# Queries and keys of a windowed attention projected three batches ahead instead of two

## The reference

```python
q = (x @ wq + bq).reshape(B, S, NH, HD)...      # 16 heads of 8; k and v likewise
for i in range(0, S, w2):                        # windows of 64 tokens, 32 apart
    qw = q[:, start:end] * scale
    attn = softmax(qw @ kw^T);  wo = attn @ vw
    out = ... blended with a linear ramp where two windows overlap
...
out = ctx @ wproj + bproj + residual             # then layer norm, gelu MLP, residual
```

## Time and profile before

| what | before |
|---|---|
| three runs, us | 391.68, 396.9, 400.08 |
| median, us | 396.9 |
| profiled execution, us | 393.26 |
| its span, us | 391.5 |
| PE busy | 298.5 us, 76% |
| DVE busy | 226.1 us, 58% |
| ACT busy | 141.4 us, 36% |
| POOL busy | 78.1 us, 20% |
| DMA, moved | 22.98 MB, mean 59 GB/s |
| granted PE clock, mean | 0.80 |

### The profile page before, as it was taken

One profiled execution on the slowest core, in us unless ns is written; L12 is line 12 of the kernel. 1 busy time (PEld: TensorE's weight loads), 2 busy tenths in 40 slices (PEclk: granted clock), 3 DMA queues, 4 the chain that ended last, 5 costly groups with the idle time before them and its releaser, 6 DMA issues.

```text
span 391.5 us, 10964 instructions
## 1 busy us (share of the span) xinstructions
PE 298.5 (76%) x4194; PEld 232.2 (59%) x4194; DVE 226.1 (58%) x632; ACT 141.4 (36%) x282; POOL 78.1 (20%) x116
## 2 busy tenths in 40 slices
PE   6363769848769958657576687689889798999993
PEld 4132646736547836536455576556558687878893
DVE  6453506617525426428227254256888689879886
ACT  2243034235314334415322413516544622742310
POOL 4343002203103104104002001003353002302020
PEclk9865587688855568959857856869989899999998
DMA  6019370470650650731812905100000000000000
GB/s 181 14 46 188 78 130 2 126 99 4 145 79 4 140 82 5 174 47 43 167 18 74 150 3 183 43 1 2 0 2 1 0 3 0 28 1 0 28 27 29
DMA packets 39057, 22.98 MB, mean 59 GB/s; under 512 B 4832, under 2 KB 37984, under 8 KB 39008
## 3 DMA queue, kind: packets, MB, share of 16 engines
q1 hardware_dynamic: 39008, 22.28, 27.1%
HBM read 13.88 MB, written 8.13 MB: 56 GB/s over the span
## 4 chain that ended last, share of the span: by engine, by line
PE 38%; DVE 17%; DMA 16%; SPq 13%; issue 10%; ACT 3%; POOL 1%; DVEq 0%; ACTq 0%; POOLq 0%
DMA qst<-stack_scratch 11%; SPq L279 5%; DMA stack_scratch<-parts 5%; SPq L299 5%; PE bank L400 5%; PE bank L658 5%; SPq L291 3%; DVE xh L1027 3%; PE bank L640 3%; PE bank L439 3%; DVE acc L1358 2%; PE bank L641 2%; PE bank L642 2%; PE bank L369 2%; PE bank L492 2%
## 5 line engine op out<-in xcount | busy, mean ns | idle before, releaser
L1068 DVE TENSOR_REDUCE nm<-bank 128x8 f32<-128x512 f32 x64 | 43.2, 688 | 71.1 <-PE bank L400 70.8
L400 PE MATMUL bank<-kst,qst 48*64 48x64 bf16 x1024 | 35.7, 226 | 43.2 <-DMA qst<-stack_scratch 30.8
L400 PEld LDWEIGHTS bank<-kst,qst 48*64 48x64 bf16 x1024 | 28.7, 136 | 57.4 <-issue 56.5
L875 POOL TENSOR_TENSOR rs<-ve,mhalf 128x2 f32<-128x2 f32 (+1 forms) x24 | 19.9, 828 | 169.7 <-DVE ve L1024 162.5
L741 ACT ACTIVATE prob<-bank 128x512 f32<-128x512 f32 x64 | 36.7, 601 | 31.6 <-PE bank L416 31.3
L658 PEld LDWEIGHTS bank<-wds,hh 128*128 128x128 f32 x256 | 32.3, 191 | 7.2 <-issue 5.6
L416 PE MATMUL bank<-qst,kst 50*64 50x64 bf16 x1024 | 29.6, 207 | 8.5 <-issue 4.7
L658 PE MATMUL bank<-wds,hh 128*128 128x128 f32 x256 | 33.7, 277 | 2.9 <-DVE acc L1358 2.4
L827 ACT ACTIVATE sg<-bank 128x512 f32<-128x512 f32 x32 | 19.0, 600 | 45.0 <-PE bank L642 45.0
L1358 DVE SCALAR_TENSOR_TENSOR acc<-bank,rt,acc 128x128 f32<-128x128 f32 x112 | 32.6, 340 | 1.1
L416 PEld LDWEIGHTS bank<-qst,kst 50*64 50x64 bf16 x1024 | 23.6, 120 | 13.8 <-issue 11.5
(11 more groups left out here) (140 smaller groups left out, 508.0 us busy)
## 6 DMA issues: line engine op xcount, KB each, us to landing
qst<-stack_scratch SPq DMA_DIRECT2D x32, 192.0 KB, 4.9
stack_scratch<-parts SPq DMA_DIRECT2D x16, 216.0 KB, 2.5
kst<-stack_scratch SPq DMA_DIRECT2D x16, 216.0 KB, 4.9
stack_scratch<-parts SPq DMA_DIRECT2D x16, 144.0 KB, 2.3
stack_scratch<-parts SPq DMA_DIRECT2D x16, 72.0 KB, 2.7
qst<-mt SPq DMA_DIRECT2D x64, 4.0 KB, 2.2
out_x<-fin SPq DMA_DIRECT2D x4, 256.0 KB, 2.3
xs<-in_x SPq DMA_DIRECT2D x1, 896.0 KB, 7.7
```

What stands on the lines that cost most here:

```text
L400: m = pe.matmul(psa[g % 2][WIN * half:WIN * half + WIN, WIN * h2:WIN * h2 + WIN], qst[n][eo][rows_, h2, at - 32 * eo:at - 32 * eo + WIN], ...
L1068: dve.tensor_reduce(nm[:, g, :], psa[g % 2][:].rearrange("p (h k) -> p h k", h=H2), AX_X, ALU.max, negate=True).then_inc(max_done, 1)
```

## The change

Queries and keys are projected three batches ahead, into three sets of stacks (`DEEP = 3`). In step b, `transpose_x`, `project_qk`, `copy_xt`, `copy_qk`, `cut_qk`, `copy_x1v` and `write_parts` work on batch b + 3; `read_stacks` and `project_v` stay at batch b + 2; the layer norm moves to b + 4. The prologue takes over the projection of batch 2 and the norm of batch 3. On SP the read now stands between the two writes of maxima, and the write of parts behind them. The scratch tensor gets an order in which the eight heads of one row of a stack lie in one run (the columns of wq and wk are permuted on the host to suit), and the query stacks keep all 288 columns. The maxima are transposed as two blocks of 32 rows and written as runs of 256 columns. All eight steps are written out, the counters kept for the loop go, and of 13 added matmuls a step 9 stay (20 become 10 in the prologue). `h3t` and `hh` share memory with the stacks. `ln2_stats` stands before `normalise(b, 0)`.

```diff
 TERMS = 6
+DEEP = 3
...
+        mp = sb("mp", [P, 2, 2, 2, H2], BF16)
+        mt = sb("mt", [4 * H2, S], BF16)
         prob = [sb(f"prob{i}", [P, H2, 2, WIN]) for i in range(2)]
         pvs = sb("pvs", [P, 4, P])
...
             vb = [attention.enter_context(nc.sbuf_tensor(f"vb{i}", [P, 2, NH, 2, 2, VC], F32)) for i in range(2)]
-            qst = [[attention.enter_context(nc.sbuf_tensor(f"qst{i}{eo}", [P, H2, S], BF16)) for eo in range(2)]
-                   for i in range(2)]
-            kst = [attention.enter_context(nc.sbuf_tensor(f"kst{i}", [P, H2, LINE], BF16)) for i in range(2)]
+            qst = [[attention.enter_context(nc.sbuf_tensor(f"qst{i}{eo}", [P, H2, LINE], BF16)) for eo in range(2)]
+                   for i in range(DEEP)]
+            kst = [attention.enter_context(nc.sbuf_tensor(f"kst{i}", [P, H2, LINE], BF16)) for i in range(DEEP)]
...
-        scr = nc.dram_tensor("stack_scratch", [B, P, TERMS, 2, LINE], BF16, kind="Internal").ap()
-        scr_rows = scr.rearrange("b (r h d) t k n -> b r k (d t) h n", r=2, h=H2)
+        scr = nc.dram_tensor("stack_scratch", [B, 2, TERMS, P, LINE], BF16, kind="Internal").ap()
...
             def write_parts(b):
                 sp.wait_ge(parts_step, after(parts_step, 3 * (b + 1)))
-                apart(sp)
-                dst = scr[ds(b, 1)].rearrange("b p t k n -> (b p) t k n")
                 for t0, n, k, src in ((0, 3, 0, parts[:, 0:1, 0, :].broadcast_to([P, 3, LINE])),
...
                                       (5, 1, 1, parts[:, 0:1, 1, :])):
-                    sp.dma_start(dst[:, t0:t0 + n, k, :], src).then_inc((q_written, k_written)[k], 16)
-
...
+                    dst = scr[b, k].rearrange("t p n -> p t n")
+                    sp.dma_start(dst[:, t0:t0 + n, :], src).then_inc((q_written, k_written)[k], 16)
+
+            def read_stacks(b):
+                n = b % DEEP
+                if b >= DEEP:
+                    sp.wait_ge(b_done, after(b_done, 8 * (b - DEEP + 1)))
+                for k, stack, written in ((0, qst[n][0], q_written), (1, kst[n], k_written),
+                                          (0, qst[n][1], q_written)):
                     sp.wait_ge(written, after(written, 48 * (b + 1)))
-                    apart(sp)
+                    rows_of = scr[b, k].rearrange("t (d h) n -> (t d) h n", h=NH)
                     for r in range(2):
-                        src = scr_rows[ds(b, 1), r, k, :, :, cols].rearrange("b r h n -> (b r) h n")
-                        sp.dma_start(stack[64 * r:64 * r + ROWS], src).then_inc(stack_ready, 16)
...
+            def write_mrow(b, hf):
                 sp.wait_ge(mt_ready, after(mt_ready, 2 * b + hf + 1))
-                apart(sp)
                 for par in range(2):
                     for part in range(2):
-                        r, at = 64 * par + ROWS + part, 32 * part + 16 * par
-                        sp.dma_start(qst[n][hf][r:r + 1].rearrange("o h (s q) -> o (h s) q", s=2),
-                                     mt[at:at + 16, :]).then_inc(mrow_ready, 16)
+                        r, at = 64 * par + ROWS + part, 16 * part + 8 * par
+                        sp.dma_start(qst[b % DEEP][hf][r:r + 1, :, 32 * hf:32 * hf + S], mt[at:at + 8, :]
+                                     ).then_inc(mrow_ready, 16)
...
+            sp.wait_ge(ones_ready, after(ones_ready, 2 * DEEP))
+            read_stacks(0)
             write_parts(1)
-            write_mrow(0, 0, 0)
-            read_stacks(1, 1)
+            write_mrow(0, 0)
+            read_stacks(1)
...
+            def step(b):
+                write_mrow(b, 1)
+                if b == 0:
+                    write_parts(2)
+                elif b + 2 < B:
+                    read_stacks(b + 2)
+                if b + 1 < B:
+                    write_mrow(b + 1, 0)
+                if b == 0:
+                    read_stacks(2)
+                if b + 3 < B:
+                    write_parts(b + 3)
+                if b == B - 2:
                     load_late()
-            steps(sp, step)
+            for b in range(B):
+                step(b)
...
+                                      qst[n][eo][rows_, h2, at:at + WIN], kst[n][rows_, h2, at:at + WIN],
                                       start=True, stop=True)
...
-                pe.transpose(bank[0:64, 0:64].bitcast(BF16), mp[:].rearrange("p a c -> p (a c)"), idb[:]
-                             ).then_inc(mt_done, 1)
-
-            def probs_v(b, n, gp):
-
-
+                for sel in range(2):
+                    m = pe.transpose(bank[0:32, 64 * sel:64 * sel + 64].bitcast(BF16),
+                                     mp[:, sel].rearrange("p c a h -> p (c a h)"), idb[:])
+                m.then_inc(mt_done, 1)
...
             pe.wait_ge(mod_ready, after(mod_ready, 2 * B))
             for g in range(5):
-                scores_a(0, 0, g)
+                scores_a(0, g)
             transpose_m(0, 0, w1b)
+            pe.wait_ge(v_ready, after(v_ready, 4))
+            transpose_x(2)
             for g in range(5, 8):
-                scores_a(0, 0, g)
-            pe.wait_ge(v_ready, after(v_ready, 4))
-            project_v(1, 1, 0)
-            project_v(1, 1, 1)
+                scores_a(0, g)
             pe.wait_ge(mt_ready, after(mt_ready, 1))
-            keep_busy(20)
-            scores_b(0, 0, 0)
-            scores_b(0, 0, 1)
...
+            project_qk(2)
+            pe.wait_ge(qk_ready, after(qk_ready, 12))
+            project_v(1, 0)
+            project_v(1, 1)
+            keep_busy(10)
+            scores_b(0, 0)
+            scores_b(0, 1)
...
+            def step(b):
+                ahead, prep, values = b + 1 < B, b + 3 < B, b + 2 < B
...
-                scores_b(b, n, 3)
+                probs_v(b, 0)
+                scores_b(b, 3)
                 a(0)
-                keep_busy(3)
+                keep_busy(2)
                 a(1)
                 if prep:
                     pe.wait_ge(v_ready, after(v_ready, 4 * (b + 2)))
-                    transpose_x(b + 2)
+                    transpose_x(b + 3)
                 a(2)
                 if not ahead:
                     turn_tokens(0)
-                probs_v(b, n, 1)
+                probs_v(b, 1)
                 if prep:
                     pe.wait_ge(att_ready, after(att_ready, b))
-                    project_qk(b + 2, n)
+                    project_qk(b + 3)
...
                 keep_busy(2)
                 a(4)
                 if ahead:
                     if prep:
-                        pe.wait_ge(qk_ready, after(qk_ready, 4 * (b + 3)))
+                        pe.wait_ge(qk_ready, after(qk_ready, 4 * (b + 4)))
...
-                probs_v(b, n, 2)
-                scores_b(b, n, 6)
-                if prep:
-                    project_v(b + 2, n, 0)
+                probs_v(b, 2)
+                scores_b(b, 6)
+                if values:
+                    pe.wait_ge(v_ready, after(v_ready, 4 * (b + 2)))
+                    project_v(b + 2, 0)
                 a(5)
...
+                scores_b(b, 7)
+                if values:
+                    project_v(b + 2, 1)
                 a(6)
...
                 a(7)
                 turn_sums(b, 1)
-                keep_busy(8)
+                keep_busy(5)
...
-                dve.tensor_copy(mt[:], (psa[0] if hf else w1b)[0:64, 0:64].bitcast(BF16)).then_inc(mt_ready, 1)
+                dve.tensor_copy(mt[:], (psa[0] if hf else w1b)[0:32, 0:128].bitcast(BF16)).then_inc(mt_ready, 1)
...
-            for n in range(2):
+            for n in range(DEEP):
...
+            ln_a(3)
             for g in range(5):
                 maxima(0, g)
             copy_mt(0, 0)
+            ln_b(3)
             for g in range(5, 8):
                 maxima(0, g)
...
+            ln_c(3)
+            cut_qk(2, 0)
+            cut_qk(2, 1)
+            ln_d(3)
...
                 maxima_next(2)
                 maxima_next(3)
-                normalise(b, 0)
                 if group is not None:
                     ln2_stats(group)
+                normalise(b, 0)
                 if norm:
...
                 if prep:
-                    cut_qk(b + 2, 0)
+                    cut_qk(b + 3, 0)
                 if ahead:
                     copy_mt(b + 1, 0)
                 if prep:
-                    cut_qk(b + 2, 1)
+                    cut_qk(b + 3, 1)
...
     vmask[P - PAD:, 1, 1] = 0
+    by_dim = np.arange(D).reshape(NH, HD).T.reshape(D)
```

More of the change, by code:

```diff
@@ L607, in step @@
                 project_out(b)
-            steps(pe, step)
+            for b in range(B):
+                step(b)
             def second(g, c):
@@ L1217, in step @@
                     ln2_stats(NG - 1)
-            steps(dve, step)
+            for b in range(B):
+                step(b)
             normed_tokens(NG - 1)
```

199 lines of the change are left out of this document (88 added, 111 removed).

## The result

| | us, median (lowest to highest, runs) | profiled execution | ratio to before, 95% interval |
|---|---|---|---|
| before | 398.49 (391.68 to 400.69, 4) | 393.26, span 391.5 | |
| after | 343.45 (339.89 to 346.75, 4) | 342.37, span 340.6 | 0.868 (0.8486 to 0.8875) |

The kernel became 13% faster: 343.45 us against 349 forecast, with a range of 335 to 366. In the profiled executions the span falls by 50.9 us: 2.3 before the first scores of batch 1 (57.55 became 55.2), 41.3 in the six steps behind it (168.05 became 126.8), and 7.3 from there to the end (165.9 became 158.6). The forecast was added up from a profiled execution: -44.3 us, beside these -50.9.

A forecast was written before the change was run, and what follows sets the result against it. The tensor engine, busy 76% of the span, waited once per step for the DMA reading the stacks. Six steps -43.1, prologue +0.3, step 6 -1.5: -44.3 from the profiled 393.26, so 349 us, range 335 to 366.

The forecast's parts named there:

- The stall: Waits of scores_a for the DMA reading the stacks, 30.8 us in seven waits; claimed gone in steps 1 to 5.
- The middle steps: Steps 1 to 4, claimed at 21.2 - 0.6 + 0.3 = 20.9 us each, with 30% of the time at the lower clock.
- The line behind it: Step time without the stall: 19.3 us plus 6.4 us times the share of time at the lower clock.
- Rival 1: Full clock everywhere: 19.0 us per middle step, 337 us in all; chance 12%.
- Not the row of maxima: Row write before scores_b(b, 4): claimed not the next wait, with 2.5 us of slack, 0.6 after a warm start.
- Rival 3: The row of maxima becomes the wait, behind the reads on SP: 2.5 us lost per step, 364 us; chance 9%.
- The chain through DVE: Vector engine from first normalisation to end of ln_d: next late, gather_context waits for it; part of the 19.3 us, kept.
- Fewer added matmuls: 13 per step become 9, before gather_context: -0.6 us a step, bounds 0 and -1.0.
- Rival 2: The clock stays low because eight matmuls before gather_context become five: 24.1 us a step, 370 us; chance 12%.
- One run per row: Stack reads move runs of eight heads at once; hidden from step 1 on, worth nothing in the sum but room.
- Step 0: Stacks of batch 2, still read in this step, arrive 22.0 us into it: +1.1 against 20.9, bounds 0 and +3.
- Behind the last first scores: Steps 6 and 7 and all behind 250 us: same work, -1.5 us for a warmer start, bounds 0 and -4.

The follow-up runs named there:

- e2: The changed kernel with projections two batches ahead, two sets of stacks and SP's old order, the rest of the change kept; 374.37 us.
- e8: The changed kernel with SP reading the stacks of batch b+2 at the end of step b, behind the part writes, in steps 1 to 5; 363.88 us.
- e6: The changed kernel with the row of maxima written in two DMAs of two rows instead of four of one row; 334.23 us.
- e9: The changed kernel with parts of batch 2 written in the prologue and the row of maxima written in two DMAs; 329.82 us.
- e3: The changed kernel with the scratch tensor in its old order, reads in runs of 576 bytes; 350.22 us.
- e7: The changed kernel with one more DVE addition of 128x512 float32 in each of the eight steps; 341.54 us.
- e12: The changed kernel with three more DVE additions of 128x512 float32 in each of the eight steps; 350.33 us.
- e4: The changed kernel with the added matmuls of before, 3, 2 and 8 a step and 20 in the prologue; 343.77 us.
- e5: The changed kernel with the parts of batch 2 written in the prologue, behind the reads of batch 1, instead of in step 0; 338.05 us.
- e1: The kernel before with its eight steps written out and nothing else changed; 391.69 us, ratio 0.9833.
- e11: The changed kernel with five more added matmuls in each step, in front of scores_a(b+1, 6); 342.03 us.

## Why the prediction was right

*The stall* went as said. No first `scores_a` of batches 1 to 7 waits for its stacks; even the exceptions named, batches 1 and 2, were none. e2 shows that the distance does it, e8 that it does so through the read's place on SP. The size was right in part by luck: -43.1 us forecast for the six steps, -41.3 measured, but the distance itself gives 34.3 of them (e2) and other parts, forecast at next to nothing, 7.0. Outside the steps -1.2 was forecast and -9.6 came.

*The middle steps* were forecast at 20.9 us and took 20.0, 20.9, 20.4 and 20.5, at 17% to 8% below full clock, which is a low share of 34, 32, 34 and 16%; 30% was assumed. The line behind it does not hold: with these shares it gives 21.5, 21.3, 21.5 and 20.3. "19.3 (never low)" was named as a bound; at full clock such a step took 17.7 and 17.6 us in e6 and 17.3 to 18.2 in e9. Some 0.8 of the difference is the write of the row of maxima (e6); the rest isn't traced. Rival 1, full clock everywhere, did not come, but its 19.0 us a step was no floor either.

*Not the row of maxima* was the step that failed, and waits of `scores_b` for it had been named as a sign of being wrong. The prediction found 2.5 us of slack, of which 0.6 would remain. In the step of 120.04 `scores_b` was ready for it 4.2 us into the step (124.80 less 0.54), not 6.5: the warm start took 2.3 of the 2.5. And the four issues took 3.21 us there, not 2.41. The waits stayed small, 4.7 us in the whole span, but they delay `turn_sums` and with it DVE's chain. A later row cost some 4 of e3's 6.8 us, an earlier one gave 9.2 (e6), part of it perhaps by the clock. Rival 3 had the mechanism, but its price of 15 us was too high.

*The chain through DVE* is late next, but with room of about 1.2 us a step (e7, e12), not at once. It has no gap worth speaking of from normalisation to `ln_d`, as forecast; what waits for it is above all `scores_a(b + 1, 6)`, up to 1.51 us a step in after, and before `gather_context` 0.6 us in the whole span.

*Fewer added matmuls*: -0.6 us a step forecast, nothing measured (e4), within the bounds given. Rival 2, a clock that stays low with fewer of them, is excluded by it: the two medians are 0.3 us apart.

*One run per row*, "worth nothing in the sum": it is worth 6.8 us (e3), 2.7 of them the prologue's first scores of batch 1. The forecast called it hidden and looked no further than the read itself; the row write beside it on the queue was the user of that time. On the size of runs the Trainium skill ("DMA: Bandwidth & Descriptors", "Specifications") names 512 B as the least transfer for line rate, which the old runs had; the landing of 6.1 us against 4.9 for the same 216 KB does not agree.

*Step 0*: 22.0 us forecast, 23.8 measured, with another cause. The stacks of batch 2 came in time. The parts of batch 2 and those of batch 3 share one buffer, and ACT waited 4.42 us for the write of the first. The prediction counted the read that moves, but not who waits for the write in front of it. e5 confirms it.

*Prologue*: +0.3 forecast, -2.3 measured. The work added is indeed covered; the reads of batch 1 land earlier, which is the layout again (57.9 us in e3). The memsets cost nothing, and POOL's first root is put down to the table of masks now, as the prediction had it:

```profile
12.03 0.71 POOL L878 TENSOR_TENSOR rs<-ve,mhalf 128x2 f32<-128x2 f32 x1 [6.90 <-DMA vmsk<-in_vmask]
```

*Written-out steps*, "0": 6.9 us by the medians (e1). The profiled executions bear out that the gap lay inside the stall, with 28.0 us for that step either way, and show 2.3 us in the whole span; by what way the rest comes is open.

*Step 5*, 19.3 forecast, 21.1 measured, at a clock of 0.68 and with a row wait of 1.82 us.

*Behind the last first scores*: -1.5 forecast, -7.3 measured, the largest miss of the sum (bounds 0 and -4). The same stretches, of before first (steps 6 and 7; then the first MLP matmuls):

```profile
225.60:258.00 32.40, 24.80 (x600) 20.18 (x600) 15.89 (x49) 10.40 (x18) 2.94 (x6) 0.66 0.21 70
258.00:293.20 35.20, 31.30 (x155) 20.86 (x152) 25.10 (x55) 17.01 (x28) 12.18 (x11) 0.90 0.00 1
...
300.30:391.50 91.20, 80.02 (x474) 68.12 (x473) 75.88 (x235) 31.12 (x51) 13.26 (x11) 0.96 0.04 12
```

and of after:

```profile
182.00:211.90 29.90, 27.24 (x606) 22.08 (x593) 16.34 (x50) 11.64 (x21) 2.92 (x6) 0.60 0.24 76
211.90:243.10 31.20, 27.39 (x149) 18.69 (x149) 23.49 (x53) 17.02 (x28) 10.96 (x10) 1.00 0.00 1
...
253.10:340.60 87.50, 78.10 (x473) 66.82 (x471) 73.86 (x234) 30.98 (x51) 11.29 (x9) 0.99 0.04 13
```

2.5 us come from steps 6 and 7, 4.0 from the MLP at full clock instead of 0.90, 3.7 from the experts; 2.9 are given back between them. e1 has the old times there (35.4 us for the MLP's part) and e2 the new ones (31.2), so it is neither the written-out steps nor the distance. Which of the remaining edits does it (memory shared with the stacks, `ln2_stats` ahead of `normalise`) was not tried, and stays open. The 5.3 us that e2's steps are shorter than e1's stay open too, as far as the layout doesn't give them. For the end the traces point to the place of `ln2_stats`: just ahead of the MLP, PE waited 2.22 us for the second norm (`xh`) in before and 3.02 in e1, and the first four MLP matmuls then took 3.78 us at the lower clock; after and e2 have no such wait, and there they took 1.98.

## What to carry to other kernels

A transfer that is hidden can still cost: ask what stands beside and behind it on its queue, and who waits for that. When work is moved a stage ahead, the place of each of its transfers in the issuing list has to move too, and every buffer it passes through is used one stage earlier. Where small DMAs lie on a chain, first count their issues: writing a row with two instead of four went with 9.2 and 8.2 us less on two kernels (after to e6, e5 to e9), while matmuls added for the clock moved the medians by at most 1.4.

## What was unexpected of the hardware

*Gaps for code in straight code.* Inside one group of matmuls PE stood still for 1.43 and 2.75 us in the kernel after and for 2.71 us in e6, and between two groups for 3.75 us in e6 (up to 89.67), with no releaser. Each time one 16 KB transfer on the instruction queue had started 2.6 to 3.0 us before the gap ended, in the last case only after the gap had begun (86.8 to 87.0). The DMA list of the kernel after for 150.4 to 150.8 us, ahead of the row of 153.40:

```profile
q8 instruction: 1, 0.02, 23.1%
```

23.1% of 16 engines in 0.4 us is 1.48 us for this one packet. That the gap is a wait for it is argued from the times alone; after has 33 such transfers, and most pass without a gap. The Trainium skill ("Runtime: NRT & Kernel Launch", "Instruction fetch mechanics") says that code comes in blocks of 16 KiB fetched ahead, mostly hidden, and that a taken branch to code outside the two blocks at hand breaks this. The loop gap of 4.08 us, gone in e1, agrees with the second. The 4.2 us of gaps in steps 0 to 5 without any branch, if they are waits for code, show that "mostly" leaves something.

*Idle pieces and the clock.* In the kernel after the granted clock fell to the lower level at 90, 111 and 131 us, each time about when PE waited for the maxima in the middle of a step. (Before 111 there was also the gap of 1.43 us.) With five matmuls there instead (e11) it stayed at the higher level from 71 to 125 us. An idle piece alone does not decide it: in step 4 of e11 PE stood still for 1.91 us up to 146.83, and the step kept 1.00.
